# Two cross-attentions of a two-layer block: another order of work per slot, and one more key batch ahead

## What is computed

```python
# layer 0 (cross 0): q, k, v with biases
scores = einsum('bhqd,bhkd->bhqk', q, k) / sqrt(16) + mask * -1e9
out = softmax(scores) @ v ; x = x + out @ Wo + bo
# layer 1 (cross 1): no mask, normalised and rotated q and k
q = apply_rope(rms_norm(q, q_norm_w), q_cos, q_sin)
k = apply_rope(rms_norm(k, k_norm_w), k_cos, k_sin)
out = softmax(q @ k.T * 16**-0.5) @ v ; x = x + out @ Wo.T
```

## Time and profile before

| | before |
|---|---|
| median of 3 runs | 1226.74 us |
| profiled execution | 1229.3 us, span 1227.3 us |
| mean granted TensorE clock | 0.889 |
| TensorE busy | 958.0 us (78%) |
| VectorE busy | 582.0 us (47%) |
| ACT busy | 455.0 us (37%) |
| GpSimd busy | 338.4 us (28%) |
| chain that ended last | PE 60%, DVE 23%, issue 7%, POOL 4%, ACT 2% |
| cross 0 | about 24 to 250 us of the span |
| cross 1 | about 594 to 953 us, with the last additions of the experts, norm and query work inside |

### The profile page before, as it was taken

How to read it: one execution, slowest core, us unless ns; L and a number is a source line. 1 busy time by engine, 2 the same in 40 slices (tenths; PEclk the granted TensorE clock), 3 DMA queues, 4 the chain that set the end, 5 groups by cost and what they waited for, 6 DMA issues and landing times.

```text
span 1227.3 us, 24260 instructions
## 1 busy us (share of the span) xinstructions
PE 958.0 (78%) x8634; PEld 758.5 (62%) x8634; DVE 582.0 (47%) x1758; ACT 455.0 (37%) x1306; POOL 338.4 (28%) x502
## 2 busy tenths in 40 slices
PE   5899999979885499999723788888877774399990
PEld 3677676744664399999512566665555653299980
DVE  4556566531554111111367687888884554022222
ACT  3566656633222032332212455655555431001000
POOL 3211112001100500000442667676662330400004
PEclk9899999989796599999957899999998765699995
DMA  8111116000000778887400000111000000789953
GB/s 255 38 36 36 36 34 232 3 1 0 1 1 1 291 297 317 324 329 272 137 14 34 26 16 32 36 36 34 0 1 2 1 1 25 271 288 327 338 198 103
DMA packets 50562, 135.76 MB, mean 111 GB/s; under 512 B 16168, under 2 KB 37552, under 8 KB 44464
## 3 DMA queue, kind: packets, MB, share of 16 engines
q1 hardware_dynamic: 47408, 126.28, 28.8%
q0 software_dynamic: 3072, 8.39, 2.0%
HBM read 117.35 MB, written 17.30 MB: 110 GB/s over the span
## 4 chain that ended last, share of the span: by engine, by line
PE 60%; DVE 23%; issue 7%; POOL 4%; ACT 2%; SPq 2%; DMA 1%; DVEq 0%; another core or an unknown queue 0%; POOLq 0%; ACTq 0%
PE lower L1000 14%; PE upper L1009 10%; PE upper L619 7%; PE upper L587 6%; PE upper L655 3%; PE lower L641 2%; PE upper L672 2%; POOL xslot L1944 2%; PE upper L780 2%; PE upper L689 2%; DVE arena L1420 2%; DVE arena L1392 1%; DVE arena L1456 1%; PE upper L959 1%; DVE x L1788 1%
## 5 line engine op out<-in xcount | busy, mean ns | idle before, releaser
L1000 PEld LDWEIGHTS lower<-arena 128*128 128x128 f32 x1472 | 175.3, 196 | 6.1 <-DVE arena L1754 3.9
L1000 PE MATMUL lower<-arena 128*128 128x128 f32 x1472 | 176.2, 279 | 2.6 <-DVE arena L1754 2.6
L619 PE MATMUL upper<-wkv,arena 128*128 128x256 f32 x512 | 141.5, 400 | 11.8 <-ACT arena L1100 6.8
L1009 PE MATMUL upper<-arena 128*128 128x256 f32 x552 | 126.4, 379 | 0.0
L1950 POOL DMA_INDIRECT arena<-yslot,slot x32 | 30.5, 953 | 323.6 <-DMA yslot<-arena 314.5
L619 PEld LDWEIGHTS upper<-wkv,arena 128*128 128x128 f32 x512 | 91.1, 193 | 34.6 <-issue 12.4
L1009 PEld LDWEIGHTS upper<-arena 128*128 128x128 f32 x552 | 101.5, 190 | 11.9
L1315 ACT ACTIVATE arena<-lower,arena 128x128 f32<-128x128 f32 x184 | 52.5, 368 | 106.6 <-PE lower L1000 106.5
L1125 ACT ACTIVATE arena<-lower,arena 128x257 f32<-128x257 f32 x128 | 59.5, 473 | 61.0 <-DVE arena L1398 61.0
L1854 POOL TENSOR_TENSOR arena<-arena 128x512 f32<-128x512 f32 x64 | 70.6, 1115 | 36.4 <-ACT klast L1178 20.9
L655 PE MATMUL upper<-const,arena 128*128 128x128 f32 x512 | 78.1, 275 | 1.7 <-ACT arena L1135 1.4
(11 more groups left out here) (231 smaller groups left out, 1743.2 us busy)
## 6 DMA issues: line engine op xcount, KB each, us to landing
arena<-in_ew_dram SPq DMA_DIRECT2D x23, 2048.0 KB, 7.1
arena<-in_ew_dram SPq DMA_DIRECT2D x23, 1536.0 KB, 6.1
arena<-in_ctxT_dram SPq DMA_DIRECT2D x16, 1028.0 KB, 5.2
xslot<-zero SPq DMA_DIRECT2D x2, 2944.0 KB, 15.2
arena<-xslot SPq DMA_DIRECT2D x46, 128.0 KB, 5.9
yslot<-arena SPq DMA_DIRECT2D x46, 128.0 KB, 6.1
const<-in_const_dram SPq DMA_DIRECT2D x1, 1151.0 KB, 7.6
x<-in_x_dram SPq DMA_DIRECT2D x1, 1024.0 KB, 5.7
```

Of the source, the lines that this page charges most:

```text
L619: ins = mm(bank[6 + w][:, 0:D], dctx[k2][:, c, j2, w * P:w * P + P], wkv[l][:, c, D:2 * D], start=(c == 0), stop=(c == KC - 1))
L1000: ins = mm(bank[1 + half][:, i * P:i * P + P], ew[k][:, at:at + P], exT[k % 2][:, c, :], start=(c == 0), stop=(c == KC - 1))
L1009: ins = mm(bank[4 + k % 2][:, 0:D], eh[k % 2][:, i, :], ew[k][:, at:at + D], start=(i == 0), stop=(i == nh - 1))
```

## The change

It does nine things, all in the two cross-attentions.

1. The output projection goes to bank 7 (before: bank 5). It stands between values 0 and weigh in slot j = 1, and values 1 of that slot waits for the addition to x.
2. In all other slots values 1 comes before weigh.
3. In cross 1 ACT copies the raw keys (8 buffers instead of 4).
4. ACT's order in a slot: turned keys first, then exponentials 0, both key copies, exponentials 1, and squares after them.
5. The inverse root is split: six steps in the slot of the odd batch's sums, six in the next slot.
6. In cross 1 TensorE turns the keys ahead of the scores.
7. VectorE merges after the maxima, and adds the projection at the slot's end, behind the norms.
8. GpSimd rotates both tiles of a batch in four instructions instead of eight.
9. Keys run 7 ahead, differ 6, sums 6, and the early part holds all slots before the last (`EARLY = 2`).

```diff
-        KEYS_AHEAD = (2, 6)
-        DIFF_AHEAD = (2, 5)
-        SUMS_AHEAD, NORM_AHEAD, ROPE_AHEAD, TURN_AHEAD = 5, 4, 3, 2
-        EARLY = 3
+        KEYS_AHEAD = (2, 7)
+        DIFF_AHEAD = (2, 6)
+        SUMS_AHEAD, NORM_AHEAD, ROPE_AHEAD, TURN_AHEAD = 6, 4, 3, 2
+        HALF_STEPS = ROOT_STEPS // 2
+        EARLY = 2
...
+                def emptied_before(n, k, j, w, kind):
+                    b = batch(n, j)
+                    n2, _, j2, _ = ahead(n, k, j, 0, TURN_AHEAD)
+                    n3, _, j3, _ = ahead(n, k, j, 0, KEYS_AHEAD[l])
+                    if kind == "values" and there(n3):
+                        pe.wait_ge(q["kc"], KW2 * batch(n3, j3) + w + 1)
+                    elif kind != "turned" and l == 1 and there(n2):
+                        pe.wait_ge(q["tc"], KW2 * batch(n2, j2) + w + 1)
+                    elif not isinstance(b, int) or b >= 0:
+                        after(pe, q["vc"], KW2 * b + w + 1)
+                    else:
+                        after(pe, q["kc"], KW2 * (batch(n3, j3) - 1) + w + 1)
...
                 def slot(n, k, j, it):
                     turns(n, k, j, it, 0)
+                    if l == 1:
+                        turn_keys(n, k, j, it, 0)
+                        turn_keys(n, k, j, it, 1)
                     scores(n, k, j, it)
-                    if there(n):
-                        project(n, k, j)
                     keys(n, k, j, it, 0)
                     turns(n, k, j, it, 1)
                     keys(n, k, j, it, 1)
-                    if l == 1:
-                        turn_keys(n, k, j, it, 0)
-                        turn_keys(n, k, j, it, 1)
                     values(n, k, j, it, 0)
-                    weigh(n, k, j, it)
-                    values(n, k, j, it, 1)
+                    if j == 1 and there(n) and not (isinstance(n, int) and n == 0):
+                        output(n - 1, k ^ 1)
+                        weigh(n, k, j, it)
+                        values(n, k, j, it, 1)
+                    else:
+                        values(n, k, j, it, 1)
+                        weigh(n, k, j, it)
...
                     act.wait_ge(q["kw"], KW2 * b2 + w + 1)
+                    if l == 1:
+                        after(act, q["kn"], b2 - 2 * QB + 1)
+                        A(kraw[k2][j2][:, w, :], bank[6 + w][:, 0:D], copy).then_inc(q["kc"], 1)
+                        return
...
                 def slot(n, k, j, it):
                     turned(n, k, j, it)
-                    squares(n, k, j, it)
-                    keys(n, k, j, it, 0)
-                    exps(n, k, j, it, 0)
-                    keys(n, k, j, it, 1)
                     turned_keys(n, k, j, it, 0)
                     turned_keys(n, k, j, it, 1)
+                    exps(n, k, j, it, 0)
+                    keys(n, k, j, it, 0)
+                    keys(n, k, j, it, 1)
                     exps(n, k, j, it, 1)
+                    squares(n, k, j, it)
                     values(n, k, j, it, 0)
...
                     if there(n2):
                         b2 = batch(n2, j2)
-                        after(dve, q["krope"], KW2 * (b2 - 1))
+                        if j2 % 2 == 0:
+                            roots(n2, j2 // 2, 1)
+                        after(dve, q["krope"], b2 - 1)
...
                 def slot(n, k, j, it):
                     n0, k0, j0, _ = ahead(n, k, j, it, -1)
+                    shares(n, k, j, it)
+                    maxima(n, k, j, it)
                     if there(n0):
                         merge(n0, k0, j0)
-                    shares(n, k, j, it)
+                    turned(n, k, j, it)
+                    if l == 1:
+                        norms(n, k, j, it)
                     if j == 1 and there(n) and not (isinstance(n, int) and n == 0):
                         added(n - 1)
-                    maxima(n, k, j, it)
-                    keys(n, k, j, it, 0)
-                    turned(n, k, j, it)
-                    keys(n, k, j, it, 1)
-                    if l == 1:
-                        norms(n, k, j, it)
```

142 lines of the change are left out of this document (60 added, 82 removed).

## The result

The changed kernel takes 1249.3 us, the median of 4 runs (1246.7 to 1252.2), against 1226.7 us for the kernel before in the same session: ratio 1.018, interval 1.015 to 1.021. It is slower, by 22.7 us; the forecast was 9.5. The profiled execution after is the lowest of its four (1246.73 us, span 1244.9), so its trace explains 17.6 us, span (1244.9) against span (1227.3).

What follows compares the result with a forecast made beforehand. TensorE was taken to bound cross 0 and VectorE cross 1. Terms of +18 (cross 0), -17.5 (cross 1) and +9 (start of cross 1) gave +9.5 on 1226.7, so 1236 us, range 1219 to 1251.

Steps and rivals of the forecast that it cites:

- Part 1, cross 0: First cross-attention: values 0 wait for key copy 0 behind the exponentials, ordinary slots 6.15 to 6.9; +18 us.
- output slot: Slot of each four-slot block holding the output projection: 7.9 us forecast in cross 0 (today 7.82), 10.1 in cross 1.
- burst slot: Cross 0 slot where GpSimd's four differ instructions run beside VectorE: from 7.21 to 8.0 us, bounds 7.5 and 8.4.
- Part 3, the start: Start of cross 1: additions start near 636 instead of 621.45, first scores' wait shortens by 4.5; +9 us in all.
- Part 2, cross 1: Second cross-attention: VectorE loses two raw-key copies per slot, a new loop sets 7.45 us slots; -17.5 us in all.
- The loop itself: Cross 1, per slot: maxima, exponentials, key copies, squares, sums, half the roots, normalised keys, reciprocal, share; taken as 7.45 us.
- signs that the forecast named: Cross 0 key-copy waits about 0.8 us; cross 1 sums wait for squares, slots near 7.6; VectorE idles 10 before L1787.
- Rival A: Cross 1: GpSimd's long rope instructions sit on the loop, 0.4 us more per slot, kernel 1249 us; chance 0.20.
- B: Rival, no difference: cross 0's burst slots cost only 7.5, the start costs 4, kernel 1227 us; chance 0.17.
- D: Rival, faster: cross 0's exponentials start earlier, the copy is never late, kernel 1218 us; chance 0.08.
- C: Rival, faster: cross 1's loop does not close, ACT runs ahead, TensorE sets the pace, kernel 1210 us; chance 0.12.

Runs made afterwards that it cites:

- run 3: Changed kernel with TensorE's and ScalarE's old orders in cross 0 alone, VectorE's new order kept: 1257.6 us.
- Run 8: Changed kernel with the whole of cross 0 as before (old orders of three engines, projection in bank 5): 1233.5 us, ratio to before 1.007.
- run 5: Changed kernel with GpSimd's rope in cross 1 on only one of sixteen heads, the rest not computed: 1222.7 us.
- runs 1: Changed kernel with GpSimd's rope of cross 1 cut back into two sets of four shorter instructions, one per key tile: 1256.7 us.
- run 4: Changed kernel with the early part of cross 1 ended two slots sooner (EARLY = 4 instead of 2): 1247.5 us.
- run 7: Changed kernel with VectorE's addition of the projected tile in cross 1 between sums and norm instead of behind the norm: 1245.1 us.

## Why the prediction was right in sign and wrong in size

**Part 1, cross 0: right, +16.2 for +18.** Timeline of TensorE, changed kernel:

```profile
120.35 0.69 PE L638 MATMUL lower<-arena 32*64 32x257 f32 x16
...
124.09 1.99 PE L616 MATMUL upper<-wkv,arena 128*128 128x256 f32 x8 [0.67 <-ACT arena L1080]
...
127.40 0.69 PE L638 MATMUL lower<-arena 32*64 32x257 f32 x16
...
130.89 1.99 PE L616 MATMUL upper<-wkv,arena 128*128 128x256 f32 x8 [0.43 <-ACT arena L1080]
...
134.20 0.69 PE L638 MATMUL lower<-arena 32*64 32x257 f32 x16
```

Values 0 wait 0.67 and 0.43 us for the key copy, where the forecast had them start 0.8 later, and these two ordinary slots last 7.05 and 6.80 us, where 6.9 was forecast. From scores to scores the rest of a block is 7.7 for the output slot (forecast 7.9) and 8.4 for the burst slot (forecast 8.0). The 8.4 is the forecast's own upper bound, with both additions of the merge stretched: L1437 and L1439 take 0.83 and 0.88 us at 146.31 and 147.26, beside GpSimd's differences. So the merge meets GpSimd here too, once in a block. The key copy's wait is the forecast's mechanism, but taking it away alone does not give the time back: in run 3 weigh waits for the probability copy behind the merge instead. Run 8 put back all three orders and the bank.

**Part 3, the start: right, +10.6 for +9.** From the first gather, the additions start 41.1 us later instead of 24.9: +16.1, forecast +15. The eight pairs give back 2.8 us (forecast 3). The roots of the query norm, which meet two ropes, take 3 us more (forecast 1). The chain from the last query instruction to the first scores is 5.4 shorter (8.1 for 13.4; forecast 4.5). Timeline of VectorE and TensorE:

```profile
649.07 1.00 DVE L1787 SCALAR_TENSOR_TENSOR x<-arena,gsm,x 128x256 f32<-128x256 f32 x2
...
692.99 2.29 DVE L1551 TENSOR_TENSOR xn<-outT,qT 128x2048 f32<-128x2048 f32 x1
```

```profile
701.05 0.69 PE L638 MATMUL lower<-arena 32*64 32x257 f32 x16 [0.69 <-POOL arena L1860]
```

**Part 2, cross 1: the step that failed.** It is the pair of sentences "the merge and probT copy, which fit between maxima and sums" and "GpSimd is not in the loop. [...] I add 0.2 us per slot (bounds 0 and 0.5)". The loop itself is real: with the rope nearly taken away (run 5) the slot is 7.0 to 7.3 us and the sums wait for the squares. But the merge does not fit. It takes 2.8 us beside the ropes instead of the 0.8 to 1.3 that the trace of before showed, and the last of the three ends 0.3 us after the squares would have let the sums begin; the probability copy comes on top. The surcharge is not 0.2 but 0.8 to 1.1 us per slot (7.8 to 8.35 against 7.0 to 7.3 in the same slots of run 5). From reciprocal 0 to 25 the forecast had 200 us and 5 for GpSimd; run 5 takes 198.0, the changed kernel 213.1, so GpSimd's rope costs 15.1. For the last six slots it had 37.5 and nothing for GpSimd; run 5 takes 35.4, the changed kernel 40.7, so it costs 5.3. With what was measured in place of the three parts, the sum is 9.5 + 11.2 for cross 1, less 1.8 for cross 0, plus 1.6 for the start: 20.5 us, against 22.7 by the medians.

Of the signs that the forecast named, those of cross 0 and of the start appear (waits of 0.4 to 0.7 us for the key copy; VectorE idles for 6.4 and 4.1 us ahead of two of the last three sums before L1787). In cross 1 they don't: in the ordinary slots the sums don't wait for the squares, these slots last 7.8 to 8.35 us and not near 7.6, and no slot is above 10 except where the clock has fallen. The long slot is 9.4 us, where 10.1 was forecast for the output slot.

Rival A named the mechanism and the time, 1249, and had a chance of 0.20. It let the share, the roots' first steps and the merge each wait; most of the waiting is at the merge, since in the new order the rope's two long instructions start just when the maxima end. That its time is met to the microsecond is in part luck: it had 0.6 us per slot for GpSimd in all, where 0.8 to 1.1 were measured, and the shorter loop made up for a part. The argument held against it, that maxima, sums and exponentials take no part in such waits, is true of these three, but it is beside the point. GpSimd starts its rope as soon as kn is there, so the rope lies at the same place of VectorE's row in every slot, and the merge had been moved to this place.

The Trainium skill ("SBUF — State Buffer", "Who interferes with whom") says that a VectorE instruction with two SBUF inputs waits for the whole of the GpSimd instruction that holds the shared port. The trace agrees: L1437 and L1439 end 0.08 us after L1820 and L1822, and their mean falls from 1.01 to 0.32 and 0.42 us when the rope instructions are halved. The forecast cited this rule and set it aside for the stretches of the old trace. These had been measured where the merge met rope instructions of 0.45 to 0.73 us.

B and D did not occur, for the parts 1 and 3 came at their full price. (D's 1218 lies just outside the stated range, which the forecast does not say.) C would have needed squares done before the probability copy; that did happen here, by 0.9 us, but because the copy was late, not because the squares were early.

Open: which of the three orders of cross 0 costs how much was not run one by one. Nor was the merge run in a third place, behind the probability copy or the sums. The slot after an output slot is TensorE's in the changed kernel: it is busy for all of the 9.4 us, with 115 matmuls where the slot before has 61, at a granted clock of 1.00 where it lasts 9.4.

## What to carry to other kernels

Where two engines share something, first find out what starts the other engine's long instruction: if it is an event of your own loop, the meeting is not an average but happens at the same place in every slot, and the price is the whole remainder of that instruction, less what the other chain would have waited anyway. Look at the trace of the new order, instruction by instruction, for what stands there. And count a shortened wait only after asking which wait of the same length lies behind it: runs 1, 3 and 4 each removed a true wait, and came out 7 and 8 us slower and 2 us faster.

## What the runs showed of the hardware that was not expected

VectorE's waits for GpSimd depend on the instruction's operands in a way that the forecast used only for its argument: L1437 needs 0.22 us alone (its shortest in the trace) and 1.15 beside a rope instruction, while L1434, with one operand in PSUM, keeps 0.28, the sums keep 0.67 and the maxima 0.68 beside the same work.

The granted clock fell behind waits of TensorE that lie inside an otherwise busy stage: 2.2 to 2.4 us in the output slots of the changed kernel and of runs 4 and 5, 1.6 to 2.0 in run 7, 3.05 in cross 0 of run 3. But it did not fall behind each of them, and in run 4 it fell more often than in the changed kernel behind waits of the same length. That an earlier start (run 4) or a shorter slot (run 5) brings more such falls, or a shorter wait (run 7) fewer, is each seen in one profile only and is not shown. One such fall costs 1.3 to 2.8 us of a slot, so a difference of under 5 us in cross 1 should be read slot by slot.
